# Typed projection and relation table built tile by tile in type order, with table rows stored by index

## What is computed

```python
def gt_layer(x, ntype, etype, src, dst, Wk, Wq, Wv, Wa, Watt, Wmsg, pri, skip, g, b):
    k = typed_linear(x, ntype, Wk)          # one 128x128 weight per node type
    q = typed_linear(x, ntype, Wq)
    v = typed_linear(x, ntype, Wv)
    kT = einsum('nhd,htdo->nhto', k, Watt)  # for every node and all 32 edge types
    vT = einsum('nhd,htdo->nhto', v, Wmsg)
    kw, m = kT[src, :, etype], vT[src, :, etype]
    a = sum(kw * q[dst]) * pri[:, etype].T / SQRT_D
    att = edge_softmax(a, dst, n)
    hag = segment_sum(m * att, dst)
    h = silu(typed_linear(hag, ntype, Wa))
    h = h * alpha + x * (1 - alpha)         # alpha = sigmoid(skip[ntype])
    return layernorm(h) * g + b
# two layers, then out = layernorm(x + h @ ff_w + ff_b)
```

## Time and profile before

| | us |
|---|---|
| median of three runs | 4091.22 |
| the profiled execution | 4095.23 |
| its span, first to last instruction | 4093.4 |

### The profile page before, as it was taken

How to read it: one execution, slowest core, us unless ns; L and a number is a source line. 1 busy time by engine, 2 the same in 40 slices (tenths; PEclk the granted TensorE clock), 3 DMA queues, 4 the chain that set the end, 5 groups by cost and what they waited for, 6 DMA issues and landing times. The chain is left out here.

```text
span 4093.4 us, 62881 instructions
## 1 busy us (share of the span) xinstructions
PE 2490.5 (61%) x13663; PEld 1768.1 (43%) x13664; DVE 2595.1 (63%) x6913; ACT 1587.2 (39%) x3599; POOL 2474.9 (60%) x2636
## 2 busy tenths in 40 slices
PE   0455666536666666666465656646666766666487
PEld 0222222225555555555342222225555555555465
DVE  6305556547777777777555556546777777777654
ACT  0115555513343334343334556523333343333332
POOL 3773333357777777775474333347777777777266
PEclk9867888857777777776677888866677777777555
DMA  3358999964444454444546999974455545444322
GB/s 78 114 125 346 423 414 412 417 199 136 136 135 138 132 138 133 137 133 134 113 125 251 424 414 414 417 281 137 133 137 133 138 134 135 134 135 126 81 71 54
DMA packets 305716, 804.87 MB, mean 197 GB/s; under 512 B 69459, under 2 KB 230048, under 8 KB 292894
## 3 DMA queue, kind: packets, MB, share of 16 engines
q1 hardware_dynamic: 189645, 545.43, 36.2%
q0 software_dynamic: 98384, 255.10, 22.5%
q10 hardware_dynamic: 17408, 1.08, 0.3%
HBM read 349.53 MB, written 460.43 MB: 198 GB/s over the span
## 5 line engine op out<-in xcount | busy, mean ns | idle before, releaser
L701 POOL DMA_INDIRECT region<-relation_table,key_of x1664 | 1632.9, 981 | 579.1 <-issue 504.1
L1027 PE MATMUL bank<-region,onehots 128*128 128x136 f32 x3328 | 729.7, 384 | 431.7 <-DVE region L1400 348.8
L1027 PEld LDWEIGHTS bank<-region,onehots 128*128 128x128 f32 x3328 | 621.5, 270 | 525.1 <-DVE sums L1415 290.0
L990 PE MATMUL bank<-region 128*128 128x512 bf16 x1568 | 519.1, 483 | 389.3 <-ACT region L813 314.1
L829 ACT ACTIVATE onehots<-iota_free,minus_dst 128x128 f32<-128x128 f32 x1664 | 528.7, 388 | 562.8 <-PE bank L1027 559.7
L1362 DVE COPY region<-bank 128x512 f32<-128x512 f32 x784 | 496.6, 684 | 380.8 <-DMA relation_table<-region 347.7
L1013 PE MATMUL bank<-region_q,onehotT 128*128 x4992 | 589.4, 275 | 93.0 <-DVE onehotT L1386 87.9
L1378 DVE TENSOR_TENSOR region<-bank,region 128x512 f32<-128x512 f32 x416 | 286.9, 690 | 514.1 <-DMA region<-relation_table,key_of 502.1
L1013 PEld LDWEIGHTS bank<-region_q,onehotT 128*128 128x128 bf16 x4992 | 502.2, 125 | 175.7 <-issue 114.3
L813 ACT COPY region<-bank 128x512 f32<-128x512 f32 x784 | 418.1, 602 | 373.4 <-DMA relation_table<-region 317.5
L1415 DVE TENSOR_TENSOR sums<-sums,bank 128x136 f32 x1664 | 473.4, 285 | 76.9 <-DVE sums L1415 46.5
(11 more groups left out here) (225 smaller groups left out, 2839.1 us busy)
## 6 DMA issues: line engine op xcount, KB each, us to landing
relation_table<-region SPq DMA_DIRECT2D x98, 4096.0 KB, 15.5
edge_places_in<-edge_places SPq DMA_DIRECT2D x416, 128.0 KB, 3.3
region<-relation_table,key_of POOLq DMA_INDIRECT x1664
sums<-qkv_rows SPq DMA_DIRECT2D x98, 192.0 KB, 15.4
flags<-segment_flags SPq DMA_DIRECT2D x104, 128.0 KB
region<-x_sorted SPq DMA_DIRECT2D x32, 256.0 KB, 2.9
aggregated_rows<-sums SPq DMA_DIRECT2D x6, 768.0 KB, 5.2
x_sorted<-region SPq DMA_DIRECT2D x16, 256.0 KB, 2.3
```

Of the source, the lines that this page charges most:

```text
L701: pool.indirect_dma_start(out=rows[:, block_.r, q * QUAD + s], out_offset=None, in_=table, in_offset=bass.IndirectOffsetOnAxis(ap=key_of[: ...
L990: nc.tensor.matmul(bank[2 + k % 6][:, :], x_spreadT[:, par, k, :], w_rel[:, k, :], start=True, stop=True).then_inc(table_psum, 1)
L1027: ins = nc.tensor.matmul(bank[SUM_BANK[q % 2][pair]][:, s * SUMC:(s + 1) * SUMC], onehots[:, at, 2 * pair + s], rows[:, block_.r, slot, RH ...
```

## The change

`typed(0)` and `build_table(0)` become one stage `fused(0)`, `typed(1)` and `build_table(1)` become `fused(1)`. Both work in type order throughout. `typed(2)` stays as `finish()`.

- The table is made of the 64 sorted tiles, not of 49 in node order. A tile's q, k, v go from PSUM straight to a ring of four in `kvq` (ACT, `keep_qkv`), with no trip through DRAM for k and v.
- A finished half of `stage` is stored by POOL with an indexed DMA, one 32 KB row per node (`store_table`), in place of SP's contiguous store.
- q alone is scattered to `q_dram` (`store_q`). After the fused stage SP loads it whole into `q_stage`, and ACT (12 copies) and DVE (8 subtractions) split it into the bf16 `q_parts`, ahead of `attend`.
- Each engine runs `step(tile)` in turn, starting 16 tiles early. In one step the engine does its part for tile n of the table, transposes tile n + 1, projects tile n + 3 (PE), splits tile n + 2 (POOL). The group work of layer 1 is spread over the four steps of a group.
- POOL gathers one tile per step: 16 tiles ahead in layer 1, 12 ahead in layer 0. In layer 0 the rows go to `g_hn`, which has two groups; the gather of a group's first tile waits until the group two before is transposed (`hnT_psum`). PE does that transpose (`turn_hn`) in the step three tiles ahead of the group.
- Four PSUM banks serve the table in place of six. ACT evicts nine heads (the even ones and the last), DVE seven; ACT copies one half of the transposed spread, DVE the other.
- `relation_weights(0)` and the seven `turn_slots` come earlier and in one piece. Small tensors share an `arena` in SBUF.

The core of the diff (lines left out are marked):

```diff
-        table = dram("relation_table", [NPAD * RT, TABLE_ROW], F32)
-        qkv_dram = dram("qkv_rows", [NPAD, 3 * D], F32)
+        table = dram("relation_table", [N * RT, TABLE_ROW], F32)
+        q_dram = dram("q_rows", [NPAD, D], F32)
...
# SP
+                for g in range(GROUPS):
+                    if l == 0:
+                        sp.wait_ge(gathered[g % 2], 64 * (g // 2) + 64)
+                    else:
+                        if g + 2 < GROUPS:
+                            sp.wait_ge(var_ready, g + 1)
+                            load_res(x_sorted, g + 2)
+                        sp.wait_ge(hn_ready, g + 1)
+                    sp.dma_start(group_rows(x_sorted if l == 0 else h_sorted, g), g_hn[:, g % 2]).then_inc(stored[g % 2], 16)
...
-                    sp.dma_start(table[bass.ds(c * P * RT, P * RT), :].rearrange("(p t) n -> p t n", t=RT),
-                                 stage[:, k % 2]).then_inc(table_stored[k % 2], 16)
...
+                for k, part in enumerate(AGG_PARTS):
+                    sp.dma_start(q_stage[:, part], q_dram.rearrange("(c p) d -> p c d", p=P)[:, part]).then_inc(q_in[k], 16)
...
# POOL
+                def gather_piece(tile):
+
+                    g, t = tile.g, tile.j
+                    if l:
+                        if t == 0:
+                            wait(pool, inT_psum, g - 1)
+                        gather_agg(1, g, t)
+                        return
+                    if t == 0:
+                        wait(pool, hnT_psum, g - 1)
+                        wait(pool, stored[g % 2], 16 * (g // 2))
+                    pool.indirect_dma_start(out=g_hn[:, g % 2, t], out_offset=None, in_=x,
+                                            in_offset=bass.IndirectOffsetOnAxis(ap=gather_node[:, tile.n:tile.n + 1], axis=0)
+                                            ).then_inc(gathered[g % 2], 16)
...
+                def store_table(tile):
+
+                    pool.wait_ge(stage_act, A * (l * TILES + tile.n + 1))
+                    pool.wait_ge(stage_dve, V * (l * TILES + tile.n + 1))
+                    pool.indirect_dma_start(out=table.rearrange("(n t) d -> n (t d)", t=RT),
+                                            out_offset=bass.IndirectOffsetOnAxis(ap=scatter_node[:, tile.n:tile.n + 1], axis=0),
+                                            in_=stage[:, tile.par].rearrange("p t n -> p (t n)"), in_offset=None,
+                                            bounds_check=N - 1, oob_is_err=False).then_inc(table_stored[tile.par], 16)
+
+                for at in range(-4 * GROUP, SORTED_TILES + 1):
+                    tile = Tile(0, at)
+                    if tile.shift(-1).real:
+                        store_table(tile.shift(-1))
+                    if l and tile.j == 3 and 0 <= tile.g + 2 < GROUPS:
+                        power(tile.g + 2)
+                    if tile.shift(2).real:
+                        split_kv(tile.shift(2))
+                        store_q(tile.shift(2))
+                    coming = tile.shift((4 if l else 3) * GROUP)
+                    if coming.real:
+                        gather_piece(coming)
...
# PE
+                def step(tile):
...
+                    group = lambda n: tile.shift(n * GROUP - tile.j)
...
+                    if tile.real:
+                        build(tile)
+                    if tile.j == 1 and group(1).real:
+                        turn_hn(group(1), tile)
+                    if spread.real:
+                        for half in ((1, 0) if tile.j == 1 else (0, 1)):
+                            turn_spread(spread, half)
+                    if new.real:
+                        project_qkv(new, new_types)
...
# ACT, ahead of attend
+                for m in range(3):
+                    for k, part in enumerate(AGG_PARTS):
+                        if m == 0:
+                            act.wait_ge(q_in[k], 16 * (l + 1))
+                        else:
+                            act.wait_ge(q_left, 8 * l + 4 * m + k - 3)
+                        nc.scalar.copy(q_parts[:, part, m], q_stage[:, part].bitcast(BF16)[:, :, 1::2]).then_inc(q_copied, 1)
```

More of the change, by code:

```diff
@@ L57 @@
 Z_BANK, OUT_BANK = (1, 7), (3, 4)
+IN_BANK, QKV_BANK, SPREAD_BANK, TABLE_BANK, TABLE_BANKS = 0, 1, (2, 3), 4, 4
+KV_RING = 4
+ACT_HEADS = [0, 2, 4, 6, 8, 10, 12, 14, 15]
+DVE_HEADS = [k for k in range(2 * H) if k not in ACT_HEADS]
+LOOP_TURNS = 6
 SUM_BANK = ((5, 6), (7, 0))
@@ L380, in repeat, with __init__, shift, in_turn @@
                     chain.n = start + per * count
+        class Tile:
+            def __init__(self, turn, at):
+                self.turn, self.at, self.n = turn, at, 8 * turn + at
+                self.k, self.par, self.half = at % KV_RING, at % 2, 4 * turn + at // 2
+                self.j, self.g = at % GROUP, 2 * turn + at // GROUP
+                self.gpar, self.ghalf = (at // GROUP) % 2, turn + at // (2 * GROUP)
+                self.first = isinstance(turn, int)
+                self.real = not self.first or 0 <= self.n < SORTED_TILES
+            def shift(self, n):
+                return Tile(self.turn, self.at + n)
+        def in_turn(eng, step, chain=None):
+            for at in range(-4 * GROUP, 0):
+                step(Tile(0, at))
+            def turn(i):
+                for at in range(2 * GROUP):
+                    step(Tile(i, at))
+            repeat(eng, LOOP_TURNS, turn, chain)
+            for at in range(8 * LOOP_TURNS, SORTED_TILES):
+                step(Tile(0, at))
         def group_rows(array, g):
@@ L691, in attend @@
+                        gather(g + lead)
+                    if 0 <= g - 2 < GROUPS:
+                        scatter(g - 2)
+                    power(g)
             def attend(l):
                 for par in range(2):
[L693 removed]
+                    pool.wait_ge(table_stored[par], 16 * (TILES // 2) * (l + 1))
                 def gather(block_, q):
@@ L999, in attend @@
+                for g in range(3):
+                    project(g // 2, g % 2)
+                repeat(pe, HALF_GROUPS - 2, groups)
+                for i in (HALF_GROUPS - 2, HALF_GROUPS - 1):
+                    groups(i)
             def attend(l):
```

761 lines of the change are left out of this document (408 added, 353 removed).

## The result

The changed kernel takes 4155.69 us (median of four runs, 4149.44 to 4158.6) against 4091.26 us for the kernel before, in runs on the same chip: 1.0157 times as long, with a 95% interval of 1.0139 to 1.0174. It is slower by 1.6%, where 1.1% was forecast (4137 us, range 4045 to 4235).

What follows compares the result with a forecast made beforehand. DMA engines were taken to bound the table stages, POOL attend and the stages ahead of the table. Attend's start, 80 us later in layer 0 and 34 earlier in layer 1, made 46 us longer: 4137 us, range 4045 to 4235.

Steps and rivals of the forecast that it cites:

- Layer 0, first store: Start of layer 0's table: the first table store was to come at 186 us, against 328.2 before.
- Layer 1, first store: Start of layer 1's table: the first table store was to come at 2040 us, against 2200.1 before.
- (a): Table stages: 48 tiles of 100 rows or more at 10.65 us in layer 0, 10.85 in layer 1: 511 and 521.
- (b): Table stages: eleven part-filled tiles, small ones at 7.5 us, 7.8 with small rows: 88 us in layer 0, 91 in layer 1.
- (c): End of each table: five empty tiles, the first hidden, four bound by ACT at 7.3 us, plus last landing: 33 us.
- (d): Layer 0's table: POOL's group-opening gather waits for PE's transposes, leaving DMA idle 9.1 us, 12 times: 109 us.
- (e): Ahead of attend: loading and splitting q delays first products some 20 us, hidden by POOL's 49 us of room.
- dear-store rival: POOL's indexed table stores: 32 KB rows cost 8 us instead of 1.0, about +400 us, 4500 in all; chance 0.08.
- Scattered rows: Table stores: rows scattered by node are written at 0.8 of the rate, +240 us less cover, 4340; chance 0.04.
- faster rival: Table stages: the new wait costs little and small tiles nearly nothing, 4028 or 4046 us; chance 0.19.
- Engines at the pace: Table stages: overlap fails and engines set the pace, tiles at 11 to 11.5 us, 4200 in all; chance 0.07.
- signs named in advance: Layer 0 gathers wait some 150 us; DMA share about 0.8, layer 1 near 0.9; first table gathers about 927 and 2765.

Runs made afterwards that it cites:

- the longer copies: The changed kernel with each of ACT's twelve copies of q made six times, both layers: 4197.58 us against 4153.02 (first try, slower session: 4726.3).
- the cut tiles: The changed kernel with eight full tiles of layer 1 storing only about a tenth of their rows: 4141.69 us against 4155.69.

## Why the prediction was right, and where its sizes were off

The time came out 19 us above the forecast, by the mechanism it named. By the steps of its sum, which come to 46 us where the trace has 63.4:

- **Layer 0, first store:** 186 forecast, 190.5 measured. Two things were missed. The seven slots take 2.94 us each and not 2, and end at 173. And POOL's gather of tile 8 waits 20.4 us (the row "DMA x_sorted<-arena" above) for SP's store of the first group, which stands on SP's queue behind the weights of the relations and the slots' flags; POOL's splits of the first tiles are queued behind that gather. With 10 tiles ahead it comes after the first of these splits, and the first store is at 183.1. How late that store of the first group lands varies: in the second profiled execution of the changed kernel (the session of the longer copies) the wait is 17.9 us and the first store at 186.5, so that the size of this miss is that of one execution.
- **Layer 1, first store:** 57.2 us behind the first gather forecast (2040 - 1982.8), 52.4 measured. The first group is normalised 28.2 us behind the gather and not 31.4 as before, its first split starts 4.2 later where 3 were put, and POOL's three steps with the power take 20.1 and not the 22.8 of the sum; a step without the power is 6.2, its last subtraction 1.16 where twice 0.67 was put.
- **(a), (b), (c) tiles:** with the wait gone, table 0 takes 644.2 us against 511 + 88 + 33 = 632, and table 1 655.2 against 645. So they are 10 to 12 us too small a layer. In layer 1 some 6 of the 10 are the small tiles (some 8.9 each by the cut tiles, 7.8 and 8.1 forecast), and 4 the tail: from the last full tile's store to the first table gather are 48 us, where 10.85 + 33 = 43.9 were put.
- **(d), the new wait:** 12 times, 109 us forecast. Measured: 12 long steps, 106.4 us in table 0, 8.9 each. The medians differ by 109.1 and the two profiled spans by 104.8, so the mechanism and the size hold, and that the medians give the very 109 is luck. Made in layer 1 it costs 111.7 in 11 steps, 10.2 each. The forecast's upper bound of 11 was for PE at its lower clock. In windows of 6 us that end 1 us before each of these twelve gathers PE's granted clock is 0.50 to 0.73 (1.00 in the first), and the DMA share 0.00 to 0.15. Here is the one of the step shown further up, 434 to 440, into which falls most of PE's work after an idle time of 5.4 us:

```profile
434.00:440.00 6.00, 4.46 (x11) 1.37 (x12) 4.05 (x6) 3.82 (x7) 0.00 (x0) 0.50 0.01 2
```

  A granted clock of 0.50 is the 1.2 GHz level. So PE was at it in much of these waits, and the price stayed at 8.9.
- **(e), q:** hidden, with the 49 us of room that were read from the kernel before. The trace and the run with longer copies agree.
- **POOL's store of 32 KB rows:** 1008 ns taken, 989 ns measured. The dear-store rival is out. The rule on packets in the Trainium skill (DMA: Bandwidth & Descriptors, SWDGE vs HWDGE vs iDMA: 4096 B at most "preferably") does not show as a cost here: the packets of 8 KB or more are nearly as many as rows of the table are stored (12807 and 2 x 6250), and POOL pays for a row of 32 KB what it pays for one of 1.5 KB.
- **Scattered rows:** out, by the run with contiguous ones.
- **The faster rival** wanted the wait below 5 us each; it is 9.
- **Engines at the pace:** they don't set the pace of full tiles; when the wait went, its 109 us came, and in a stretch of full tiles the DMA share is 0.99.
- **Attend and the last stage:** forecast unchanged; the two attend stages are 2.1 us longer and 1.0 shorter, the last stage 3.2 shorter.

The misses add up: 4.5 at layer 0's first store, 12.2 - 2.6 in its table (tiles and wait), -4.8 at layer 1's first store, 10.2 in its table, and 2.1 - 1.0 - 3.2 are 17.4, the 63.4 less 46. The tiles alone are 22 too small, and part of that is made good by terms that came out smaller than forecast.

The signs named in advance: gathers that wait for the transposes 14 times, 167 us, of which the 12 long ones take 165 (150 forecast; for 5 of the 14 the profile names ACT's evictions, which stand ahead of the transposes); DMA share 0.72 in layer 0's table and 0.84 in layer 1's (0.8 and 0.9 forecast, the order right and both too high); first table gathers at 941 and 2787 (927 and 2765).

What the forecast did not see is that the price hangs on one tile of distance. It named the step of PE that the gather meets, and yet judged the change as a whole. The fused stages are worth 0.9% as soon as that step is one earlier (11 tiles), and 1.1% with 10 tiles.

## What to carry to other kernels

Where one engine issues the stores of a pipeline and also prefetches for it, put the two side by side at the prefetch that waits, and ask which tile's work stands ahead of what it waits for: if it is that of the next tile, and that tile can't be finished before the last store issued has landed, the store queued behind the prefetch comes too late and the DMA queue runs dry once a turn. The cure is a distance by which the thing waited for is done in a step that the store needs in any case, or one earlier, and the check is to move the distance by one. With two buffers, a tile with few rows costs most of a full one (8.9 of 10.8 us here), so padding of a work list to whole tiles has to be priced by the step and not by its bytes.

## What the runs showed of the hardware

- POOL's DMA by index mostly costs 0.94 to 1.03 us and 0.3 to the next, whether a row has 512 B, 1 KB or 32 KB, gathered or scattered. From issue to landing its table stores take 13.7 us in the median, part-filled and empty tiles among them; SP's stores of 4 MB in the kernel before took 15.5.
- The first table gathers of attend are slow while DVE subtracts on q, two inputs in SBUF, from 942.11 to 950.81. Here are POOL's gathers, then DVE's row:

```profile
941.06 0.98 POOL L732 DMA_INDIRECT region<-relation_table,key_of  x1 [6.83 <-issue]
942.34 2.50 POOL L732 DMA_INDIRECT region<-relation_table,key_of  x1 [0.30 <-issue]
945.15 1.34 POOL L732 DMA_INDIRECT region<-relation_table,key_of  x1 [0.30 <-issue]
...
951.93 0.95 POOL L732 DMA_INDIRECT region<-relation_table,key_of  x1 [0.30 <-issue]
...
942.11 8.70 DVE L1717 TENSOR_TENSOR sums<-sums 128x1664 f32<-128x1664 f32 x5 [2.52 <-ACT region_q L927]
```

  Five gathers take 8.1 us in place of 4.8, and the sixth is at its 0.95 again. The Trainium skill (GPSIMD Engine Reference, Key points) has POOL share its SBUF interfaces with VectorE, with contention where DVE has two SBUF inputs. The trace agrees in place and time here, but not throughout: in attend DVE's products (L1585, two inputs in SBUF, 128x512, 0.68 us) often lie wholly within a gather that takes its usual 0.95, as at 1224.7. No run took the subtractions away, so the cause of the slow gathers is not shown.
- Writes of 32 KB rows go at the same rate whether the rows lie one behind the other or scattered by node over 205 MB: 402 and 404 GB/s by busy share over the stage, and 414 scattered in full tiles against 415 for SP's contiguous stores before.
- In one session the kernel before took 14% longer (4665 us), and so did the one with the longer copies (4726, 4198 in the later session). The table stages of the latter take 751 and 657 us, as elsewhere; attend is the part that grew (1404 us in layer 0 against 1155 with the same copies later). These runs and those in which the kernel before took 4098.51 us were on a chip of the same number, so it is open whether the chip or the moment made the difference. What makes it slow was not looked into.
